# Column sums of W' moved from GpSimd to TensorE, and the output bias moved into the second lora contraction

## The chip, the core and the metric

One kernel on one core of a Trainium2 chip. The metric is the device time of one execution in microseconds, the median of several runs. The engines are TensorE (PE, with its weight loads PEld), VectorE (DVE), ScalarE (ACT), GpSimd (POOL) and SyncE (SP), which here only issues DMAs. TensorE's clock is granted at one of two levels, 1.2 and 2.4 GHz.

## What is computed

x has 64 samples of 64 channels and 1024 features, cond_128 one row per sample.

```python
h = gelu(cond @ W0 + b0); h = gelu(h @ W1 + b1)
att = softmax(h @ W2 + b2)                      # 64 x 8
agg_w = einsum('bk,koi->boi', att, weight)      # per sample 64 x 64
agg_b = att @ bias_k                            # per sample 64
c = einsum('boi,bih->boh', agg_w, x) + agg_b[:, :, None]
out = einsum('bsd,od->bso', c, W) + b
scores = c @ gate_w.T + gate_b                  # 4 ranks: 8, 16, 32, 64
sel = argmax(softmax(scores))                   # top-1, weight 1
final = c @ A[:r].T @ B[:, :r].T                # r the selected rank
y = x + out + final
```

## The kernel before

W' stands for the three weights side by side, [W.T | A.T | gate_w.T], 1024 rows and 1024 + 64 + 4 = 1092 columns, in three PSUM banks of 364 columns (`CB`). The kernel swaps the order of the two linear steps: for each of 32 tiles of 128 rows (two samples) it first computes z = x W', and then mixes the rows of z by agg_w, which is laid out as a block-diagonal 128 x 128 matrix `bd`. The bias agg_b of the mixing step then becomes, in the output, agg_b of the row times the column sums of W'.

All large contractions use fp32r operands split in a high and a low part (`xth`, `xtl`, `wh`, `wl`, `zh`, `zl`, `bd` 0 and 1): ScalarE copies the high part, VectorE subtracts it for the low part, TensorE does three passes of the four. A tile is 3 banks x 8 chunks of k x 3 passes = 72 matmuls (`main`, line 634), 9 for the mixing (`mix`, lines 653, 654, 657), 6 for lora (`lora`, lines 670 and 671) and one transpose (line 662).

The route of a tile (`route`, lines 509 to 535) adds `ubias` to the last 68 columns of the mixed z, takes the running maxima of the four scores and masks the 64 lora columns; the result in two parts, `usplit`, is transposed by TensorE, copied by ScalarE (`u_transposed`, lines 393, 394) and contracted with B in two parts (`bt_h`, `bt_l`). Of the second contraction, `ut_h1` x `bt_l`, 64 rows are lora; rows 64 to 127 of `ut_h1` are ones, and `bt_l` holds b in rows 64 (high) and 96 (low) there and zeros elsewhere. `residual` (lines 483 to 494) adds x and writes y.

GpSimd does the bias. While the chunks of W' come in it adds them up: seven additions over 128 x 1092 (line 309). The sum `wsum` is split on ScalarE (line 422) and VectorE (line 594), and six matmuls with a matrix of ones (lines 735, 736, in the second bank of tile 1) bring the column sums to all partitions; ScalarE copies them to `colsum` (line 436). Per tile GpSimd then forms `ubias` (`u_bias`, lines 322, 327) and adds the bias times 1024 columns to the x in `xin` (`x_bias`, lines 332, 337), which `residual` waits for.

Each engine has its program written out by hand, and the order is that of the text. Tile 0 is done chunk by chunk of k, as W' arrives (lines 685 to 712), with the small conditioning matmuls between (after k = 1 and after k = 4), whose results stand in banks of `p_out`. In step(0, 1), tile 1, the mixing of tile 0 stands behind k = 5, 6 and 7 of the first bank, the column sums behind k = 3 of the second, the mixing of tile 1 starts at the end of the second bank and behind k = 3 of the third, and the transpose and lora of tile 0 and the transpose of tile 1 close the third. From tile 2 on, a step has the last mixing and lora of the tile before in its first bank, and a transpose behind k = 4 of its third (9 main matmuls before the next step), for whose copies the next step waits (`s_utc`). VectorE's order ahead of the loop is: the low halves of W' (`w_lo`, line 451) with the attention softmax and its copies between, `xt_lo` of tile 1, `mixing_weights` of tile 0 (product L463, sum L466), z_lo (line 480), `bd_lo`, and lines 588 to 596. SP issues all loads of tiles 0 to 3 at once and then, in its loop, the load four tiles ahead and the store of the tile.

## Time and profile before

| | us |
|---|---|
| median of 3 runs | 508.31 |
| lowest and highest run | 507.74, 508.41 |
| the profiled execution: span from its first to its last instruction | 505.8 |
| TensorE busy | 478.2 |
| VectorE busy | 272.7 |
| GpSimd busy | 190.9 |
| ScalarE busy | 125.3 |

The times of the runs hold what lies around the span too; of the profiled execution the span is what the profile gives. In the profile, busy times add up the instructions of an engine. A matmul's row gives its pipelined duration, so that the spacing of starts tells the rate. "L634" is a line of the kernel, "<-DVE zl" in brackets who ended the idle time before an instruction. The granted clock is 1.00 at 2.4 GHz and 0.50 at 1.2 GHz.

### The profile page before, as it was taken

Reading aid. Unit: us, or ns where it says so; the run is one execution under the profiler, and the core shown is the slowest. Engines: PE = TensorE matmul, PEld = TensorE weight load, DVE = VectorE, ACT = ScalarE, POOL = GpSimd, SP = SyncE. Lnnn points to the kernel's source line nnn. Section 1 sums busy time; section 2 is a strip of 40 time slices with the busy share of each in tenths; the row PEclk is TensorE's granted clock in tenths of the full one; section 3 lists DMA queues with packets and bytes.
Section 4 is the critical chain, followed back from the end, with each engine's and each line's share of the span. In section 5 each row is a group of like instructions: output and inputs, shape, how many; then the busy total and the mean of one; then the engine's idle time right before and its main releaser. Section 6 shows DMA issues by size and latency. Waiting matters only on the chain.

```text
span 505.8 us, 8213 instructions
## 1 busy us (share of the span) xinstructions
PE 478.2 (95%) x2837; PEld 472.5 (93%) x2837; DVE 272.7 (54%) x665; ACT 125.3 (25%) x275; POOL 190.9 (38%) x149
## 2 busy tenths in 40 slices
PE   5578689999999999999999999999999999999996
PEld 4567589999999999999999999999999999999996
DVE  4999985445455544454555445445554454455523
ACT  6415112222212222222122222221222212122211
POOL 4994953333332233333322333332223333322200
PEclk9799799999999999999999999999999999999999
DMA  8940052233333223333322233333222333321002
GB/s 291 351 162 1 1 180 97 101 126 125 124 124 110 74 68 121 124 124 124 124 90 78 80 124 124 124 124 124 77 83 88 124 124 124 124 83 41 29 14 84
DMA packets 16270, 55.91 MB, mean 111 GB/s; under 512 B 2050, under 2 KB 2818, under 8 KB 16260
## 3 DMA queue, kind: packets, MB, share of 16 engines
q1 hardware_dynamic: 16116, 55.71, 31.2%
q8 instruction: 6, 0.10, 0.1%
q10 hardware_dynamic: 144, 0.07, 0.1%
q14 instruction: 4, 0.03, 0.0%
HBM read 39.00 MB, written 16.78 MB: 110 GB/s over the span
## 4 chain that ended last, share of the span: by engine, by line
PE 87%; DVE 9%; issue 1%; DMA 1%; ACT 1%; SPq 0%; POOL 0%; DVEq 0%; ACTq 0%; POOLq 0%
PE p_z L634 70%; PE p_out L653 3%; PE p_out L657 3%; PE p_out L654 3%; PE p_out L671 3%; PE p_out L670 3%; DVE wl L451 1%; DVE prod L463 1%; DVE xtl L457 1%; DMA b2r<-in_b 1%; DVE um L526 1%; PE p_out L634 1%; DVE bd L472 1%; PE p_z L662 1%; DVE xtl L558 1%
## 5 line engine op out<-in xcount | busy, mean ns | idle before, releaser
L634 PE MATMUL p_z<-wh,xth 128*128 128x364 f32 x752 | 251.5, 334 | 3.5 <-ACT wh L363 2.0
L634 PE MATMUL p_z<-wl,xth 128*128 128x364 f32 x752 | 248.0, 330 | 3.9 <-DVE wl L451 3.9
L634 PE MATMUL p_z<-wh,xtl 128*128 128x364 f32 x752 | 248.2, 330 | 0.0
L480 DVE TENSOR_TENSOR zl<-p_z,zh 128x364 fp32r<-128x364 f32 x94 | 50.4, 536 | 198.5 <-ACT zh L385 198.5
L634 PEld LDWEIGHTS p_z<-wh,xth 128*128 128x128 f32 x752 | 142.1, 189 | 5.8 <-ACT wh L363 2.2
L634 PEld LDWEIGHTS p_z<-wl,xth 128*128 128x128 f32 x752 | 141.9, 189 | 4.4 <-DVE wl L451 4.4
L634 PEld LDWEIGHTS p_z<-wh,xtl 128*128 128x128 f32 x752 | 142.4, 189 | 0.0
L327 POOL TENSOR_TENSOR ubias<-wsum,gbias 128x68 f32<-128x68 f32 x32 | 10.7, 333 | 256.8 <-DVE usplit L535 256.5
L385 ACT ACTIVATE zh<-p_z 128x364 fp32r<-128x364 f32 x94 | 44.7, 475 | 188.1 <-PE p_z L634 188.0
L337 POOL TENSOR_TENSOR xin<-xin,wsum 128x1024 f32<-128x1024 f32 x32 | 77.6, 2426 | 3.7 <-POOL wsum L332 2.3
L332 POOL TENSOR_TENSOR wsum<-colsum,aggb 128x1024 f32<-128x1024 f32 x32 | 60.7, 1898 | 0.7
L457 DVE TENSOR_TENSOR xtl<-xtin,xth 128x1024 fp32r<-128x1024 f32 x31 | 41.1, 1327 | 15.3 <-ACT xth L370 15.3
L653 PE MATMUL p_out<-zh,bd 128*128 128x364 f32 x96 | 32.2, 336 | 9.5 <-DVE zl L480 7.1
L370 ACT ACTIVATE xth<-xtin 128x1024 fp32r<-128x1024 f32 x31 | 32.9, 1060 | 1.4 <-DMA xtin<-in_xt 0.7
L657 PE MATMUL p_out<-zl,bd 128*128 128x364 f32 x96 | 31.7, 331 | 0.0
L654 PE MATMUL p_out<-zh,bd 128*128 128x364 f32 x96 | 31.7, 330 | 0.0
L393 ACT ACTIVATE ut_hl<-p_z 128x128 fp32r<-128x128 f32 x32 | 8.9, 278 | 91.5 <-PE p_z L662 91.5
L671 PE MATMUL p_out<-bt_l,ut_h 128*128 128x364 f32 (+1 forms) x96 | 31.0, 323 | 0.0
L670 PE MATMUL p_out<-bt_h,ut_hl 128*128 128x364 f32 (+1 forms) x96 | 30.3, 324 | 0.0
L377 ACT ACTIVATE bd<-aggw 64x64 fp32r<-64x64 f32 x32 | 8.2, 256 | 84.9 <-DVE aggw L466 84.9
L653 PEld LDWEIGHTS p_out<-zh,bd 128*128 128x128 f32 x96 | 18.1, 189 | 10.7 <-DVE zl L480 6.2
L490 DVE TENSOR_TENSOR wraw<-p_out,xin 128x728 f32<-128x728 f32 x31 | 28.1, 905 | 0.0
(92 smaller groups left out, 373.0 us busy)
## 6 DMA issues: line engine op xcount, KB each, us to landing
xin<-in_x SPq DMA_DIRECT2D x32, 512.0 KB, 4.5
xtin<-in_xt SPq DMA_DIRECT2D x31, 512.0 KB, 5.0
out<-wraw SPq DMA_DIRECT2D x31, 512.0 KB, 3.0
wraw<-in_wag SPq DMA_DIRECT2D x8, 546.0 KB, 7.5
bt_raw<-in_bt SPq DMA_DIRECT2D x2, 256.0 KB
xtin<-in_xt SPq DMA_DIRECT2D x1, 384.0 KB, 5.3
out<-wraw SPq DMA_DIRECT2D x2, 182.0 KB, 2.2
kern<-in_kernels SPq DMA_DIRECT2D x2, 128.0 KB, 11.1
```

The lines of the kernel that those rows point to most:

```text
L332: nc.gpsimd.tensor_tensor(bias[:, 0:O], colsum[:, 0:O], aggb[:, t, :].broadcast_to([P, O]), ALU.mult).then_inc(s_bias_x, 1)
L337: nc.gpsimd.tensor_tensor(xs, xs, bias[:, 0:O], ALU.add).then_inc(s_xb, 1)
L370: nc.scalar.activation(xth[:, j % 2, :], xtin[:, j % UNROLL, :], ACT.Copy).then_inc(s_xth, 1)
L385: nc.scalar.activation(zh[:, ring(j, m), :], z_place(i, j, m), ACT.Copy).then_inc(s_zh, 1)
L457: nc.vector.tensor_tensor(xtl[:, j % 2, :], xtin[:, j % UNROLL, :], xth[:, j % 2, :].bitcast(F32), ALU.subtract).then_inc(s_xtl, 1)
L480: nc.vector.tensor_tensor(zl[:, at, :], z_place(i, j, m), zh[:, at, :].bitcast(F32), ALU.subtract).then_inc(s_zl, 1)
L634: last = nc.tensor.matmul(z_place(i, j, m), a[:, q, k * P:(k + 1) * P], w[:, k, n * CB:(n + 1) * CB], start=k == 0 and p == 0, stop=k == K ...
L653: nc.tensor.matmul(o, bd[:, q, 0, :], zh[:, at, :], start=opens, stop=False, skip_group_check=not opens)
L654: nc.tensor.matmul(o, bd[:, q, 1, :], zh[:, at, :], start=False, stop=False, skip_group_check=not opens)
L657: nc.tensor.matmul(o, bd[:, q, 0, :], zl[:, at, :], start=False, stop=True, skip_group_check=not opens).then_inc(s_mix, 1)
L670: nc.tensor.matmul(o, ut_hl[:, :], bt_h[:, cols], start=opens, stop=False, skip_group_check=True)
L671: last = nc.tensor.matmul(o, ut_h1[:, :], bt_l[:, cols], start=False, stop=True, skip_group_check=True)
```

## The change

GpSimd's additions of W', the split of their sum, the six column-sum matmuls of tile 1 and `x_bias` go. In place of them:

- In the first loop over k, TensorE multiplies a matrix of ones with `wh` and with `wl` of each chunk, in three banks each: 3 x 2 x 8 = 48 matmuls, into the three banks that the mixing of tile 0 uses later. The conditioning results move to the one bank left free, `p_out[:, 1, 2]`.
- The column sums' 68 lora and gate columns are copied to `colsum` as before; row 0 of the other 1024 is split into `cs_h` (ScalarE) and `cs_l` (VectorE) before the mixing of tile 0 may overwrite the banks (`s_cs_lo`).
- agg_b is computed a second time in transposed form (two more small matmuls), split into `aggbt_h` and `aggbt_l`, and brought by three DMAs into rows of `ut_rows`, an array that has for each tile five rows: two of ones, two of the high and one of the low part of agg_b.
- Five row DMAs bring b (high, low) and the column sums (high, low, high) into rows 64 to 68 of `bt_l`. The second lora contraction takes 69 rows instead of 128, the last five being b and agg_b times the column sums; a third ScalarE copy per tile brings the five rows from `ut_rows` to `ut_h1`.
- `residual` adds x as it was loaded. GpSimd keeps the memsets, among them a new one of 2 x 4096, and `ubias`.
- `bt_raw` and `brow` now lie over chunks 2 and 3 of `wraw`, so that SP waits for the low half of chunk 3 before it loads B and b, and with them all loads behind; the first x load has moved ahead of that wait.
- On ScalarE `bd_hi(0, 0)` and the high parts of b and B move ahead of the first z_hi; on VectorE `bd_lo(0, 0)` and `mixing_weights(0, 1)` move ahead of the first z_lo.

The diff, cut to its core; the left-out lines declare buffers and semaphores, and remove `x_bias` and the additions whole:

```diff
...
     UNROLL = 4
-    ROW_BH, ROW_BL = 64, 96
+    ROW_BH, ROW_BL, ROW_GH, ROW_GL, ROWS = 64, 65, 66, 68, 69
...
-        bt_raw = sb("bt_raw", [P, O])
-        brow = sb("brow", [P, O])
+        bt_raw = wraw[:, 2, 0:O]
+        brow = wraw[32:33, 3, 0:O]
+        b_h, b_l = cs_h[32:33, :], cs_l[32:33, :]
...
+        ps_cond = p_out[:, 1, 2, :]
+        ps_h1 = ps_cond[:, 0:NB]
...
+        ps_aggbt = p_z[0:T, 1, 0:P]
...
                 sp.dma_start(kern[h, :, :], kernels).then_inc(s_kern_in, 16)
-            sp.wait_ge(s_clear, 2)
+            sp.wait_ge(s_clear, 1)
             sp.dma_start(gbias[:, R:RE], gate_b.partition_broadcast(P)).then_inc(s_gate_in, 16)
-            for r in (ROW_BH, ROW_BL):
-                sp.dma_start(brow[r:r + 1, :], b.rearrange("(a o) -> a o", a=1)).then_inc(s_lora_in, 16)
+            sp.dma_start(xin[:, 0, :], x_t[0]).then_inc(s_x_in[0], 16)
+            sp.wait_ge(s_wl, 4)
+            sp.dma_start(brow[:, :], b.rearrange("(a o) -> a o", a=1)).then_inc(s_brow_in, 16)
...
                 sp.dma_start(bt_raw[h, :], bt).then_inc(s_lora_in, 16)
-            sp.dma_start(xin[:, 0, :], x_t[0]).then_inc(s_x_in[0], 16)
...
+            sp.wait_ge(s_aggbt, 1)
+            for r in (ROW_GH, ROW_GH + 1):
+                sp.dma_start(ut_rows[r:r + 1, :, :], aggbt_h[:, :].bitcast(F32)).then_inc(s_gate_rows, 16)
+            sp.wait_ge(s_aggbt, 2)
+            sp.dma_start(ut_rows[ROW_GL:ROW_GL + 1, :, :], aggbt_l[:, :].bitcast(F32)).then_inc(s_gate_rows, 16)
+            sp.wait_ge(s_b_hi, 1)
+            sp.dma_start(bt_l[ROW_BH:ROW_BH + 1, :].bitcast(F32), b_h.bitcast(F32)).then_inc(s_rows, 16)
+            sp.wait_ge(s_b_lo, 1)
+            sp.dma_start(bt_l[ROW_BL:ROW_BL + 1, :].bitcast(F32), b_l.bitcast(F32)).then_inc(s_rows, 16)
+            sp.wait_ge(s_cs_hi, 1)
+            for r in (ROW_GH, ROW_GL):
+                sp.dma_start(bt_l[r:r + 1, :].bitcast(F32), cs_h[0:1, :].bitcast(F32)).then_inc(s_rows, 16)
+            sp.wait_ge(s_cs_lo, 1)
+            sp.dma_start(bt_l[ROW_GH + 1:ROW_GH + 2, :].bitcast(F32), cs_l[0:1, :].bitcast(F32)).then_inc(s_rows, 16)
...
             nc.gpsimd.memset(gbias[:, :], 0.0).then_inc(s_clear, 1)
-            nc.gpsimd.memset(brow[:, :], 0.0).then_inc(s_clear, 1)
+            nc.gpsimd.memset(ones_r[:, :].bitcast(F32), 1.0).then_inc(s_clear, 1)
             nc.gpsimd.memset(bd[:, :, :, :].bitcast(F32), 0.0).then_inc(s_clear, 1)
-            nc.gpsimd.memset(ut_h1[:, :].bitcast(F32), 1.0).then_inc(s_clear, 1)
-            nc.gpsimd.memset(ones_r[:, :].bitcast(F32), 1.0).then_inc(s_clear, 1)
...
+            pool.wait_ge(s_clear, 3)
+            nc.gpsimd.memset(ut_rows[ROW_BH:ROW_GH, :, :], 1.0).then_inc(s_clear, 1)
...
             pool.wait_ge(s_aggb, 1)
-            pool.wait_ge(s_colsum, 1)
-            pool.wait_ge(s_b_lo, 1)
+            pool.wait_ge(s_clear, 4)
+            pool.wait_ge(s_cs_hi, 1)
             u_bias(0, 0)
-            u_bias(0, 1)
-            x_bias(0, 0)
-            def step(i, j):
-                x_bias(i, j)
-                if precedes(i, j):
-                    u_bias(i, j + 1)
-            run(pool, step, 2)
+            run(pool, u_bias, 1)
...
                 nc.scalar.activation(ut_hl[:, :], src, ACT.Copy)
-                nc.scalar.activation(ut_h1[0:R, :], src[0:R, :], ACT.Copy).then_inc(s_utc, 1)
+                nc.scalar.activation(ut_h1[0:R, :], src[0:R, :], ACT.Copy)
+                nc.scalar.activation(ut_h1[R:ROWS, :], ut_rows[R:ROWS, i * UNROLL + j, :], ACT.Copy).then_inc(s_utc, 1)
...
             xt_hi(0, 1)
-            act.wait_ge(s_clear, 4)
+            act.wait_ge(s_clear, 3)
+            bd_hi(0, 0)
+            act.wait_ge(s_brow_in, 16)
+            nc.scalar.activation(b_h[:, :], brow[:, :], ACT.Copy).then_inc(s_b_hi, 1)
+            act.wait_ge(s_lora_in, 16 * 2)
+            nc.scalar.activation(bt_h[:, :], bt_raw[:, :], ACT.Copy).then_inc(s_bt_hi, 1)
...
             z_hi(0, 0, 1)
-            bd_hi(0, 0)
-            act.wait_ge(s_lora_in, 16 * 4)
-            nc.scalar.activation(bt_h[:, :], bt_raw[:, :], ACT.Copy).then_inc(s_bt_hi, 1)
+            act.wait_ge(s_colsum_mm, 1)
+            nc.scalar.activation(colsum[:, :], p_out[:, 0, 2, CB - RE:CB], ACT.Copy)
+            nc.scalar.activation(cs_h[0:1, 0:2 * CB].rearrange("p (a n) -> p a n", n=CB), p_out[0:1, 0, 0:2, 0:CB], ACT.Copy)
+            nc.scalar.activation(cs_h[0:1, 2 * CB:O], p_out[0:1, 0, 2, 0:CB - RE], ACT.Copy).then_inc(s_cs_hi, 1)
             z_hi(0, 0, 2)
-            nc.scalar.activation(bt_l[R:P, :], brow[R:P, :], ACT.Copy).then_inc(s_bt_hi, 1)
-            act.wait_ge(s_wsum, KC - 1)
-            nc.scalar.activation(wsum_h[:, :], wsum[:, :], ACT.Copy).then_inc(s_wsum_hi, 1)
...
-                    act.wait_ge(s_colsum_mm, 1)
-                    nc.scalar.activation(colsum[:, :].rearrange("p (a n) -> p a n", n=CB), p_out[:, 1, :, 0:CB],
-                                         ACT.Copy).then_inc(s_colsum, 1)
...
                 if not follows(i, j, 2):
+                    act.wait_ge(s_clear, 4)
+                    act.wait_ge(s_gate_rows, 16 * 3)
...
                 dve.wait_ge(s_lora, i * UNROLL + (j + 1))
-                dve.wait_ge(s_xb, i * UNROLL + (j + 1))
+                dve.wait_ge(s_x_in[j % UNROLL], i * 16 + 16 * (j // UNROLL + 1))
...
                 dve.wait_ge(s_stored[q], 16 * (T // 2 - 1))
-                dve.wait_ge(s_xb, T)
+                dve.wait_ge(s_x_in[slot], 16 * (T // UNROLL))
...
             nc.vector.tensor_copy(aggb[:, :, 0], ps_aggb).then_inc(s_aggb, 1)
+            nc.vector.tensor_copy(aggbt_h[:, :], ps_aggbt).then_inc(s_aggbt, 1)
+            dve.wait_ge(s_aggbt, 1)
+            nc.vector.tensor_tensor(aggbt_l[:, :], ps_aggbt, aggbt_h[:, :].bitcast(F32), ALU.subtract).then_inc(s_aggbt, 1)
...
             mixing_weights(0, 0)
-            z_lo(0, 0, 0)
-            z_lo(0, 0, 1)
-            bd_lo(0, 0)
+            dve.wait_ge(s_b_hi, 1)
+            nc.vector.tensor_tensor(b_l[:, :], brow[:, :], b_h[:, :].bitcast(F32), ALU.subtract).then_inc(s_b_lo, 1)
...
                                     ALU.subtract).then_inc(s_bt_lo, 1)
+            bd_lo(0, 0)
+            mixing_weights(0, 1)
+            z_lo(0, 0, 0)
+            z_lo(0, 0, 1)
+            dve.wait_ge(s_cs_hi, 1)
+            nc.vector.tensor_tensor(cs_l[0:1, 0:2 * CB].rearrange("p (a n) -> p a n", n=CB), p_out[0:1, 0, 0:2, 0:CB],
+                                    cs_h[0:1, 0:2 * CB].bitcast(F32).rearrange("p (a n) -> p a n", n=CB), ALU.subtract)
+            nc.vector.tensor_tensor(cs_l[0:1, 2 * CB:O], p_out[0:1, 0, 2, 0:CB - RE], cs_h[0:1, 2 * CB:O].bitcast(F32),
+                                    ALU.subtract).then_inc(s_cs_lo, 1)
             z_lo(0, 0, 2)
-            mixing_weights(0, 1)
-            dve.wait_ge(s_wsum_hi, 1)
-            nc.vector.tensor_tensor(wsum_l[:, :], wsum[:, :], wsum_h[:, :].bitcast(F32),
-                                    ALU.subtract).then_inc(s_wsum_lo, 1)
...
                     nc.tensor.matmul(o, ut_hl[:, :], bt_h[:, cols], start=opens, stop=False, skip_group_check=True)
-                    last = nc.tensor.matmul(o, ut_h1[:, :], bt_l[:, cols], start=False, stop=True,
+                    last = nc.tensor.matmul(o, ut_h1[0:ROWS, :], bt_l[0:ROWS, cols], start=False, stop=True,
...
+            def column_sums(k, w):
+                for n in range(BANKS):
+                    last = nc.tensor.matmul(p_out[:, 0, n, 0:CB], ones_r[:, :], w[:, k, n * CB:(n + 1) * CB],
+                                            start=k == 0 and w is wh, stop=k == KC - 1 and w is wl)
+                return last
+            pe.wait_ge(s_clear, 2)
...
                     main(0, 0, m, k, (0, 1))
+                column_sums(k, wh)
...
                     main(0, 0, m, k, (2,))
+                sums = column_sums(k, wl)
...
                     for d in range(2):
-                        last = nc.tensor.matmul(ps_aggb[d * C:(d + 1) * C, :], bk[:, :], attt[:, d, :],
+                        nc.tensor.matmul(ps_aggb[d * C:(d + 1) * C, :], bk[:, :], attt[:, d, :], start=True, stop=True)
+                    for d in range(2):
+                        last = nc.tensor.matmul(ps_aggbt[:, d * C:(d + 1) * C], attt[:, d, :], bk[:, :],
...
                     last.then_inc(s_cond_mm, 1)
+            sums.then_inc(s_colsum_mm, 1)
...
             pe.wait_ge(s_aggb, 1)
+            pe.wait_ge(s_aggbt, 2)
...
                         main(i, j, m, k)
+                        if first and m == 0 and k == KC - BANKS:
+                            pe.wait_ge(s_cs_lo, 1)
...
                             mix(0, 0, k - (KC - BANKS))
-                        if first and m == 1 and k == 3:
-                            pe.wait_ge(s_clear, 5)
-                            pe.wait_ge(s_wsum_lo, 1)
-                            for n in range(BANKS):
-                                cols = slice(n * CB, (n + 1) * CB)
-                                o = p_out[:, 1, n, 0:CB]
-                                nc.tensor.matmul(o, ones_r[:, :], wsum_h[:, cols], start=True, stop=False)
-                                last = nc.tensor.matmul(o, ones_r[:, :], wsum_l[:, cols], start=False, stop=True)
-                            last.then_inc(s_colsum_mm, 1)
...
                         if first and m == 1 and k == 7:
-                            pe.wait_ge(s_colsum, 1)
...
                             pe.wait_ge(s_bt_lo, 1)
-                            pe.wait_ge(s_b_lo, 1)
+                            pe.wait_ge(s_rows, 16 * 5)
...
```

## Rows read from the trace of the kernel before

**Rows 1.** The page, part 1: busy us (share), instructions

```profile
PE 478.2 (95%) x2837; PEld 472.5 (93%) x2837; DVE 272.7 (54%) x665; ACT 125.3 (25%) x275; POOL 190.9 (38%) x149
```

**Rows 2.** Waits of TensorE, 0 to 75 us: total, times, longest

```profile
PE p_out L653 <- DVE zl L480: 7.1, 3, 5.2
PE p_z L634 <- DVE wl L451: 3.9, 1, 3.9
```

**Rows 3.** Windows: stretch, us, busy (xcount) of PE, PEld, DVE, ACT, POOL; PEclk, DMA, GB/s

```profile
7.60:12.60 5.00, 4.96 (x15) 4.32 (x15) 4.90 (x6) 4.77 (x7) 3.36 (x2) 1.00 1.02 410
...
54.00:60.80 6.80, 5.24 (x18) 5.16 (x19) 6.60 (x14) 0.43 (x2) 6.39 (x6) 0.51 0.00 1
...
75.00:134.00 59.00, 59.00 (x359) 58.89 (x358) 29.35 (x81) 13.72 (x32) 20.90 (x18) 1.00 0.33 114
```

**Rows 4.** Timeline of TensorE: start us, duration, line, tiles, count, idle before

```profile
26.00 0.65 PE L709 MATMUL p_out<-attd,ones 64*64 64x256 f32 x4
...
30.80 0.50 PE L634 MATMUL p_out<-wl,xth 128*128 128x364 f32 x2
...
38.42 0.41 PE L653 MATMUL p_out<-zh,bd 128*128 128x364 f32 x1 [2.42 <-DVE bd L472]
...
44.59 0.41 PE L735 MATMUL p_out<-wsum_h,ones_r 128*128 128x364 f32 x1 [1.46 <-DVE wsum_l L594]
...
55.56 0.67 PE L653 MATMUL p_out<-zh,bd 128*128 128x364 f32 x1 [5.24 <-DVE zl L480]
...
61.92 0.43 PE L634 MATMUL p_z<-wh,xth 128*128 128x364 f32 x1
...
71.71 0.43 PE L653 MATMUL p_out<-zh,bd 128*128 128x364 f32 x1 [1.52 <-DVE zl L480]
...
77.29 0.27 PE L662 MATMUL p_z<-ident,usplit 128*128 128x128 f32 x1
...
91.81 0.27 PE L662 MATMUL p_z<-ident,usplit 128*128 128x128 f32 x1
```

**Rows 5.** Timelines of VectorE, last row GpSimd, 0 to 80 us

```profile
8.04 1.28 DVE L451 TENSOR_TENSOR wl<-wraw,wh 128x1092 fp32r<-128x1092 f32 x1
...
12.92 3.57 DVE L451 TENSOR_TENSOR wl<-wraw,wh 128x1092 fp32r<-128x1092 f32 x1
...
32.58 3.02 DVE L463 TENSOR_TENSOR prod<-kern,attp 128x512 f32<-128x512 f32 x1
...
40.22 0.68 DVE L463 TENSOR_TENSOR prod<-kern,attp 128x512 f32<-128x512 f32 x1
...
48.63 1.93 DVE L526 SCALAR_TENSOR_TENSOR um<-u,pmax 128x8 f32<-128x8 f32 x1
...
54.98 0.52 DVE L480 TENSOR_TENSOR zl<-p_z,zh 128x364 fp32r<-128x364 f32 x1
...
73.17 0.23 DVE L514 TENSOR_TENSOR u<-p_out,ubias 128x68 f32<-128x68 f32 x1
...
75.00 0.54 DVE L480 TENSOR_TENSOR zl<-p_z,zh 128x364 fp32r<-128x364 f32 x1 [0.16 <-ACT zh L385]
...
12.32 25.64 POOL L309 TENSOR_TENSOR wsum<-wsum,wraw 128x1092 f32<-128x1092 f32 x6
```

**Rows 6.** Timeline of ScalarE

```profile
17.14 1.11 ACT L363 ACTIVATE wh<-wraw 128x1092 fp32r<-128x1092 f32 x1 [0.24 <-DMA wraw<-in_wag]
...
77.85 0.26 ACT L394 ACTIVATE ut_h<-p_z 64x128 fp32r<-64x128 f32 x1
```

**Rows 7.** Groups by line and form: count, busy us, mean ns, idle before

```profile
L490 DVE TENSOR_TENSOR wraw<-p_out,xin 128x728 f32<-128x728 f32 x31 | 28.1, 905 | 0.0
...
L327 POOL TENSOR_TENSOR ubias<-wsum,gbias 128x68 f32<-128x68 f32 x32 | 10.7, 333 | 256.8 <-DVE usplit L535 256.5
...
L418 ACT ACTIVATE bt_h<-bt_raw 128x1024 fp32r<-128x1024 f32 x1 | 1.1, 1057 | 0.0
```

**Rows 8.** DMA issues: count, KB, median us to landing

```profile
gbias<-in_gate_b SPq DMA_DIRECT2D x1, 2.0 KB, 10.8
```

60 lines of the change are left out of this document (21 added, 39 removed).

## The prediction

> **What bounds the kernel now.** I read the page first: TensorE is busy 478.2 of 505.8 us, everything else half of that or less [rows 1]. So time can come only from TensorE's own work, from its clock, or from the few stretches in which it stands still. The waits of TensorE tell where those are: all of them lie before 75 us, after that none is listed, and the longest end in VectorE's hands: 7.1 us for zl, 3.9 for wl [rows 2], and in the timeline 2.42 for bd before 38.42 and 1.46 for wsum_l before 44.59 [rows 4]. From 75 us on the loop is pure TensorE: the stretch 75 to 134 is busy 59.00 of 59.00 us, and the transposes of two consecutive tiles start at 77.29 and 91.81, 14.52 us apart, for 87 matmuls and one transpose, which is 0.166 us per 364-column matmul [rows 3, 4]. Nothing that the change does to GpSimd in that loop is worth anything by itself; only the first 72 us can give.
>
> **The clock.** In the windows the stretch 7.6 to 12.6 holds 15 matmuls in 4.96 us, over 0.30 each, which is the 1.2 GHz level, although the granted clock says 1.00 there; the record seems to begin without a first entry, so I go by spacing in that stretch. After the stall of 5.24 us that ends at 55.56 the clock is 0.51 over 54.0 to 60.8, the 1.2 GHz level, and the stretch from 75 on has 1.00 [rows 3, 4]. Work that resumed at 55.56 thus ran slow for 5.3 us. The idle of 2.4 us before 38.42 cost no clock: the matmul behind it took 0.41, the one behind 55.56 took 0.67 [rows 4]. For the changed kernel, which keeps TensorE busy from 7.6 on, I estimate the rise at 7.6 + 5.3, that is 13.0.
>
> **Why VectorE is late.** The split of one chunk of W' took 1.28 us at 8.04, before GpSimd's sums had begun, and 3.57 at 12.92, while GpSimd's additions ran, six of them in 25.64 us from 12.32 on. The product of kern and attp took 3.02 at 32.58 and 0.68 at 40.22, when they had ended; one masking instruction of 8 columns took 1.93 at 48.63 beside the bias products of GpSimd [rows 5]. I read this as the two engines holding each other up, and cost VectorE in the changed kernel at its undisturbed durations.
>
> **The change, part by part.**
> First loop over k. Added: two times three column-sum matmuls for each of 8 chunks, 48 in all, so 120 instead of 72. Removed: the 3.9 us wait for wl [rows 2] and a shorter one for att. From 7.6 to 13.0 at 0.30 each some 17.5 matmuls are done; the other 102.5 at 0.166 take 17.0 us; the small conditioning matmuls in the loop take 1.2 in all (the last four instructions 0.65 [rows 4]; I add 0.55 for the rest and the two new ones, by size). The loop ends at 31.2, against 31.3 before (0.50 from 30.80) [rows 4]. W' is no limit: ScalarE split the last chunk at 17.14, for 1.11 us [rows 6]. So 48 matmuls are hidden by time that was lost before, in stalls and at half clock. Without that cover they cost 8.0 us at full clock and 14.5 at half.
>
> From the loop to the first mixing matmul. Before, it starts at 38.42 [rows 4]. In the changed kernel it waits for cs_lo, because the sums stand in the banks that it overwrites. VectorE's chain sets this. The conditioning matmuls end 75 matmuls into the loop: 13.0 + 57.5 x 0.166 + 1.2 = 23.8. Then on VectorE: the copies and the split of the transposed bias 0.9, w_lo(7) 1.2, xt_lo 1.2, product and sum 1.4: 28.5. ScalarE's two bd halves 0.5 and the b row 1.06 (1024 columns, taken as independent of the partitions): 30.1 [rows 7]. VectorE again: b_l 1.2, bt_l 1.2, bd 0.45, weights of tile 1 1.4, two z_lo at 0.45 pitch 0.9, cs_l 0.9 for 728 columns and 0.4 for 296: 36.6 (the product 0.68, z_lo 0.52, a chunk of 1092 columns 1.28 and so 1024 in 1.2, 728 columns out of PSUM 0.905) [rows 5, 7]. TensorE is ready at 31.2 + 18 x 0.166 = 34.2 and stands 2.4 us, as long as the wait for bd before, which cost no clock. The mixing starts at 36.7: **1.7 us** gained. ScalarE's cs_h rows (0.8 + 0.4, after two z_hi) are done by 33.3 and hide beside VectorE.
> The one price no row shows is GpSimd beside VectorE in that chain: its first ubias pair, two instructions of about 0.33 us [rows 7], falls at 33.3, beside the weights of tile 1. In the row at 32.58 such a product lost 2.3 us to GpSimd instructions of 4.3 us each [rows 5]; a pair of 0.33 can hold it up for 0.6 at most, and not at all if it comes behind the product. I take 0 and keep 0.6 as the other end. The Trainium skill, "SBUF — State Buffer", section "Who interferes with whom", holds that a VectorE instruction with two SBUF inputs and a GpSimd instruction that reads SBUF exclude each other for the whole instruction, so that the later one blocks; by that the gain would be 1.1 us instead of 1.7 here. The same section would leave z_lo, with one input in PSUM, undisturbed, and the trace agrees: 0.52 at 54.98, between slowed neighbours [rows 5].
>
> From the first mixing matmul to the end of tile 1 (61.92 before, so 23.5 us [rows 4]). The work left there is 69 matmuls at 0.166 (11.5), one lora contraction 0.95, two transposes 0.2: 12.7. What goes: the stall at 44.59 of 1.5 us and the six column-sum matmuls 1.0; the stall of 5.2 us at 55.56; the half clock behind it, about 2.7 us. The 5.2 us stall was the route of tile 0, whose masking ran on VectorE at 48.63 and ahead of the z_lo that started at 54.98; undisturbed a route takes 1.7 us (from 73.17 to the z_lo at 75.00, less its 0.16 of idle) [rows 5]. By my walk z_lo(0, 1, 1) ends at about 45 where TensorE asks for it at 45.4: just in time, which is the tightest point of the forecast. ScalarE's third copy for the transposed u adds 0.2 to 0.3: the wait before tile 2 becomes 0.4. Sum 13.1 instead of 23.5: **10.4 us** gained, tile 1 ends at 49.8.
> From there to the mixing of tile 2 at 71.71 (9.8 us before [rows 4]): 39 matmuls and a lora contraction, 7.4. The waits of 0.3 and 1.5 for zl go with GpSimd's x_bias. **2.4 us**.
>
> The loop. The third ScalarE copy is 5 x 128. Nearest row: 64 x 128, 0.26 us [rows 6]. The transpose starts at 77.29 and its two copies end at 78.11 [rows 4, 6]; nine matmuls stand between the transpose and the wait, so the next weight load is due at about 78.7. So 0.6 us of slack cover 0.26, for all 30 tiles; if the copy took 1.06 like the 1024-column one, 0.46 x 30 = 14 us would be lost. I take 0. The contraction over 69 rows instead of 128 streams the same columns and loads the same 128 weight columns; no row has 69. The nearest, four instructions over 64 rows with 256 columns in 0.65 us, leave 0.05 each over their columns [rows 4]. I take 0; the upper end is rival 4, a gain is excluded by the unchanged columns. The residual waits for x, which landed tiles earlier: 0.
> Queues. SP now stands until wl(3), about 14.9, with b, bt and five loads for tiles 1 to 3 behind it; before, it went on at once. W' is still arriving until 17, so this delays them by a few microseconds; bt is asked for at 30, the tile 2 load at about 37. After that SP waits in turn for aggbt, b and the sums, with eight row DMAs; queued behind them are only the load for tile 4 and the first store, due at about 50. The last row is issued at 37.3 and asked for at 47. gbias, as small, took 10.8 us to land behind a full queue [rows 8]; here the queue is empty. Cost 0; at worst 1.1 us.
> New memset on GpSimd: the row of ones (2 x 4096) takes a few us of an idle engine and is asked for at 46: 0.
>
> **Sum.** 1.7 + 10.4 + 2.4 = 14.5 us. Span 505.8 - 14.5 = 491.3. The span is 2.5 us below the median of the runs, 508.31; what lies outside it stays, so 508.31 - 14.5 = **493.8 us**.
>
> **The rivals.**
> (1) A part of the stalls stays (15%). Speaks for it: z_lo(0, 1, 1) and cs_lo come on single long chains, and every 0.1 us of VectorE counts. If 3 us remain without loss of clock the time is 496.8; if the idle again costs the clock (2.7 us more), 499.5.
> (2) The clock stays at half through the first loop (5%). The loop then ends at 7.6 + 120 x 0.30 + 1.2 = 45, the mixing starts at 48, 11.5 us later than forecast: 505.3. Against it: the rise 5.3 us after 55.56 [rows 3, 4].
> (3) The change doesn't bring VectorE back (3%): its long instructions have another cause than GpSimd. Then the stall of 5.2 us stays and 48 matmuls come on top: + 8.0, less some 2.3 of the wl stall that they fill, less 2.5 of the old sums and their wait, + 3.2: 511.5, slower. Against it: the pairs at 8.04 and 12.92, 32.58 and 40.22 [rows 5].
> (4) Slower: the 69-row contraction breaks the hiding of weight loads (3%). Place: the 96 matmuls of the second lora contraction. It decides against the change from 14.5 / 96 = 0.15 us each. A weight load takes about as long as a matmul's 0.166; with one exposed before and one behind each, 96 x 0.33 = 32 us and the time 526, with one, 510. Against it: the 0.05 us over 64 rows above.
> (5) A row DMA lands late (6%): 493.8 + 1.1 = 494.9.
> The forecast as it stands has 68%.
>
> **How the numbers follow.** The range from 491.3 (the 2.4 us wait for cs_lo gone) to 499.5 (rival 1 with its clock) takes in the forecast, rivals 1 and 5, the 0.6 us of the shared port and the 0.45 us for every us that the clock rises later. About 2 in 10 are left outside. A measurement of this kernel can tell 0.2%, 1.0 us. Faster 0.93 (the forecast and rivals 1, 2 and 5, less 0.01), the same 0.01 (rival 2 or 4 coming out between), slower 0.06 (rivals 3 and 4).
>
> **What would show it.** Right: no PE wait on wl in the first loop; matmul spacing there 0.30, then 0.166 from about 13; loop end near 31; one wait of 2 to 3 us before the first mixing matmul, put down to cs_l; no wait over 0.5 us for zl after it; granted clock 1.00 from 13 on; VectorE's split of a W' chunk at 1.28 throughout; the transposes 14.52 apart in the loop. Wrong: a loop period over 14.6 (ScalarE's copy or the 69 rows), a first mixing matmul after 38, or a second stretch at half clock.

## The result, and the profile after

| | before | after |
|---|---|---|
| median (runs), us | 508.36 (4) | 492.98 (4) |
| lowest and highest | 507.74, 508.81 | 492.56, 494.87 |
| span of the profiled execution | 505.8 | 490.4 (its own time 492.56) |

The ratio is 0.9705 (95% interval 0.9687 to 0.9723): 15.4 us less. Forecast were 493.8, and 491.3 to 499.5.

Part 1 of the page after, and two groups of its part 5, which answer to [rows 1] and to the second lora contraction:

```profile
PE 477.5 (97%) x2883; PEld 473.8 (97%) x2883; DVE 248.2 (51%) x669; ACT 133.7 (27%) x308; POOL 25.8 (5%) x76
...
L665 PE MATMUL p_out<-bt_l,ut_h 69*128 69x364 f32 (+1 forms) x96 | 30.6, 319 | 0.0
...
L664 PE MATMUL p_out<-bt_h,ut_hl 128*128 128x364 f32 (+1 forms) x96 | 29.9, 320 | 0.0
```

GpSimd went from 190.9 us busy to 25.8. TensorE has more matmuls than before and is busy no longer: up to the transpose of tile 2 it was busy 53.8 us for 267 instructions before, at a mean granted clock of 0.91, and 54.2 us for 313 after, at 1.00. The loop behind it became 1.15 us shorter, as shown below. 69 rows take what 128 rows take (319 and 320 ns).

The waits of TensorE after, for [rows 2] (total, times, longest):

```profile
PE p_out L671 <- DMA cw<-in_layer: 2.9, 1, 2.9
PE p_z L628 <- ACT wh L350: 2.6, 1, 2.6
PE p_out L647 <- DVE cs_l L587: 2.2, 1, 2.2
...
PE p_z L628 <- ACT ut_h L382: 0.3, 1, 0.3
```

The 7.1 us for zl and the 3.9 for wl are gone. What comes before the first matmul of the loop is no news; behind it the wait for `cs_l` is the only large one, and the largest of the rest is 0.3. TensorE's timeline after, the marks that answer to [rows 4]; the start of the loop over k stands first:

```profile
8.20 0.64 PE L628 MATMUL p_z<-wh,xth 128*128 128x364 f32 x1 [2.56 <-ACT wh L350]
...
9.85 0.51 PE L628 MATMUL p_out<-wh,xtl 128*128 128x364 f32 x1
...
11.06 0.48 PE L628 MATMUL p_z<-wl,xth 128*128 128x364 f32 x1
11.37 0.51 PE L628 MATMUL p_out<-wl,xth 128*128 128x364 f32 x2
11.71 0.66 PE L682 MATMUL p_out<-wl,ones_r 128*128 128x364 f32 x3
12.21 0.32 PE L628 MATMUL p_z<-wh,xth 128*128 128x364 f32 x1
...
31.38 0.33 PE L628 MATMUL p_z<-wh,xth 128*128 128x364 f32 x1
...
36.73 0.43 PE L647 MATMUL p_out<-zh,bd 128*128 128x364 f32 x1 [2.21 <-DVE cs_l L587]
...
50.24 0.43 PE L628 MATMUL p_z<-wh,xth 128*128 128x364 f32 x1 [0.34 <-ACT ut_h L382]
...
57.71 0.33 PE L647 MATMUL p_out<-zh,bd 128*128 128x364 f32 x1
...
63.19 0.27 PE L656 MATMUL p_z<-ident,usplit 128*128 128x128 f32 x1
...
483.12 0.27 PE L656 MATMUL p_z<-ident,usplit 128*128 128x128 f32 x1
```

Up to 11.37 the matmuls start 0.30 to 0.31 us apart. The two from 11.37 on take 0.17 each until the next start, the three from 11.71 on (12.21 - 11.71) / 3 = 0.167, so from 11.37 on they run at full clock: the clock rose 3.2 us after the loop began. Against before, the mark of the first mixing is earlier by 38.42 - 36.73 = 1.7, the start of tile 2 by 61.92 - 50.24 = 11.7, its mixing by 71.71 - 57.71 = 14.0, its transpose by 77.29 - 63.19 = 14.1. The last transpose of the run stood here before:

```profile
498.37 0.27 PE L662 MATMUL p_z<-ident,usplit 128*128 128x128 f32 x1
```

It is earlier by 15.25. So 1.15 us more came in 29 tiles of the steady loop: one tile took (498.37 - 77.29) / 29 = 14.520 before and (483.12 - 63.19) / 29 = 14.480 after. The last 0.15 lie in the end.

VectorE's timeline after, up to the first mixing, for [rows 5], and under it GpSimd's:

```profile
4.92 1.24 DVE L530 CAST xth<-xtin 128x256 fp32r<-128x256 f32 x1 [3.95 <-DMA xtin<-in_xt]
...
11.17 1.29 DVE L439 TENSOR_TENSOR wl<-wraw,wh 128x1092 fp32r<-128x1092 f32 x1
...
30.32 1.22 DVE L576 TENSOR_TENSOR cs_l<-wraw,cs_h 1x1024 fp32r<-1x1024 f32 x1 [1.73 <-ACT cs_h L403]
31.57 1.22 DVE L578 TENSOR_TENSOR bt_l<-wraw,bt_h 64x1024 fp32r<-64x1024 f32 x1
...
33.19 0.69 DVE L451 TENSOR_TENSOR prod<-kern,attp 128x512 f32<-128x512 f32 x1
...
35.41 0.89 DVE L585 TENSOR_TENSOR cs_l<-p_out,cs_h 1x728 fp32r<-1x728 f32 x1
36.23 0.44 DVE L587 TENSOR_TENSOR cs_l<-p_out,cs_h 1x296 fp32r<-1x296 f32 x1
```

```profile
2.50 3.50 POOL L321 MEMSET ut_rows<- 2x4096 f32 x1
33.31 0.73 POOL L328 TENSOR_TENSOR bias<-colsum,aggb 128x68 f32<-128x68 f32 x1 [27.31 <-ACT cs_h L411]
...
34.63 0.30 POOL L328 TENSOR_TENSOR bias<-colsum,aggb 128x68 f32<-128x68 f32 x1 [0.18 <-POOL ubias L333]
```

Splits of W' take 1.3 and products 0.7. The low halves of b and B stand ahead of the two that write the sums' low half (L585, L587), for which TensorE waits. The first cast took 1.24 (0.29 before), while the new memset ran on GpSimd.

### The profile page after: what moved, and what is told of

Same layout as the page of the kernel before. It is cut to its first block, busy times and chain, and to the rows that moved or that the text cites. A ratio compares the mean times of both kernels' runs of the same rounds, so it can differ in the third digit from the quotient of the medians.

```text
span 490.4 us, 8228 instructions
## 1 busy us (share of the span) xinstructions
PE 477.5 (97%) x2883; PEld 473.8 (97%) x2883; DVE 248.2 (51%) x669; ACT 133.7 (27%) x308; POOL 25.8 (5%) x76
## 4 chain that ended last, share of the span: by engine, by line
PE 95%; DVE 2%; DMA 1%; ACT 1%; issue 0%; SPq 0%; DVEq 0%; ACTq 0%
PE p_z L628 76%; PE p_out L647 3%; PE p_out L651 3%; PE p_out L648 3%; PE p_out L664 3%; PE p_out L665 3%; PE p_out L628 1%; PE p_out L682 1%; DMA wraw<-in_wag 1%; PE p_z L656 1%; DVE aggw L454 0%; DVE prod L451 0%; DVE wl L439 0%; DVE bt_l L578 0%; DVE cs_l L576 0%; DVE xtl L445 0%
## 5 line engine op out<-in xcount | busy, mean ns | idle before, releaser
L445 DVE TENSOR_TENSOR xtl<-xtin,xth 128x1024 fp32r<-128x1024 f32 x31 | 38.0, 1225 | 15.9 <-ACT xth L357 15.9
L333 POOL TENSOR_TENSOR ubias<-bias,gbias 128x68 f32<-128x68 f32 x32 | 10.6, 331 | 392.7 <-DVE usplit L523 392.5
L665 PE MATMUL p_out<-bt_l,ut_h 69*128 69x364 f32 (+1 forms) x96 | 30.6, 319 | 0.0
L454 DVE TENSOR_REDUCE aggw<-prod 128x64 f32<-128x512 f32 x32 | 22.0, 686 | 1.1
L451 DVE TENSOR_TENSOR prod<-kern,attp 128x512 f32<-128x512 f32 x32 | 21.9, 685 | 0.0
```

Source lines behind the costliest of these rows:

```text
L445: nc.vector.tensor_tensor(xtl[:, j % 2, :], xtin[:, j % UNROLL, :], xth[:, j % 2, :].bitcast(F32), ALU.subtract).then_inc(s_xtl, 1)
L454: nc.vector.reduce_sum(aggw[:, :], prod[:, :, :], AX_X).then_inc(s_aggw, 1)
L665: last = nc.tensor.matmul(o, ut_h1[0:ROWS, :], bt_l[0:ROWS, cols], start=False, stop=True, skip_group_check=True)
```

## The experiments

Ratios are against the kernel before, timed on the same chip as the experiment. "After" is the changed kernel. Theory M: VectorE is held up by GpSimd's instructions, and its delay is what TensorE waited for.

**1. Additions back.** Seven additions of W' on GpSimd, over 64 partitions and into an unused part of an array, in the kernel after.

```diff
+            for k in range(1, KC):
+                pool.wait_ge(s_wh, k + 1)
...
+                nc.gpsimd.tensor_tensor(spare[:, :], left, wh[0:C, k, :].bitcast(F32), ALU.add).then_inc(s_spare, 1)
```

> The changed kernel with seven additions over 1092 columns put back on GpSimd, beside the first loop, over wh (64 partitions, same length per partition), result unused. Theory (GpSimd and VectorE hold each other up): VectorE's split of a W' chunk goes from 1.28 us to 2 to 3.6 in places, the product for tile 0 to about 3, the wait before the first mixing matmul grows from 2.2 us by 3 to 6, the time from 493 to 496 to 500 us. Rival (VectorE's long instructions before had another cause, such as the loads still landing): VectorE's durations stay, the time stays within 0.5 us of 493.

Measured: 502.66, ratio 0.9891 (0.9870 to 0.9912). That is slower than the 496 to 500 expected. Nothing of what TensorE needs was touched, and 9.7 of the 15.4 us are gone. VectorE's timeline of this kernel, then TensorE's:

```profile
11.42 3.65 DVE L450 TENSOR_TENSOR wl<-wraw,wh 128x1092 fp32r<-128x1092 f32 x1
...
15.17 2.30 DVE L563 TENSOR_SCALAR att<-expo,sm 64x8 f32<-64x8 f32 x1
...
30.40 3.56 DVE L456 TENSOR_TENSOR xtl<-xtin,xth 128x1024 fp32r<-128x1024 f32 x1
33.88 3.04 DVE L462 TENSOR_TENSOR prod<-kern,attp 128x512 f32<-128x512 f32 x1
```

```profile
45.78 0.67 PE L658 MATMUL p_out<-zh,bd 128*128 128x364 f32 x1 [6.91 <-DVE cs_l L598]
```

The split is back at 3.65 and the product at 3.04, against 3.57 and 3.02 in [rows 5]. The first mixing is 9.05 us later than after and runs at half clock (0.67). Of the 9.05 us, 4.7 are a longer wait for `cs_l`, which stands at the end of a chain of VectorE instructions: `xtl` and `prod` alone lost 4.7 us, one behind the other. The other 4.35 had been lost before, in the first loop, where TensorE waited 1.2 us for `att` and 1.1 for wl and the granted clock was 0.87 from 13 to 20 us and 0.93 from 20 to 31. This part the expectation had not counted.

**2. Bias products back.** Per tile one multiplication and one addition over 1024 columns, on 64 partitions and into an unused part of an array.

```diff
+                nc.gpsimd.tensor_tensor(spare[:, 0:O], wh[0:C, 0, 0:O].bitcast(F32), aggb[0:C, 0, :].broadcast_to([C, O]),
+                                        ALU.mult).then_inc(s_spare, 1)
+                pool.wait_ge(s_spare, t + 1)
+                nc.gpsimd.tensor_tensor(spare[:, 0:O], spare[:, 0:O], wh[0:C, 1, 0:O].bitcast(F32),
+                                        ALU.add).then_inc(s_spare_b, 1)
```

> The changed kernel with a product and a sum over 1024 columns per tile put back on GpSimd (64 partitions, result unused, nobody waits for them). Theory: the two routes in tile 1 stretch from 1.6 us to 3 to 7, a wait for zl before the mixing of tile 1's second bank comes back with 2 to 5 us, perhaps with a stretch at half clock behind it, and the time is 496 to 502 us; the loop's period doesn't change, 14.48 us, since VectorE has slack there. Rival (the route was slow for another reason): no wait for zl over 0.5 us, 493 us.

Measured: 497.74, ratio 0.9787 (0.9766 to 0.9809), 4.8 us more than after. The timelines of TensorE and VectorE:

```profile
49.88 0.43 PE L669 MATMUL p_out<-zh,bd 128*128 128x364 f32 x1 [2.60 <-DVE zl L490]
```

```profile
40.75 2.15 DVE L482 TENSOR_TENSOR bd<-aggw,bd 64x64 fp32r<-64x64 f32 x2 [0.82 <-ACT bd L387]
...
43.39 2.98 DVE L467 TENSOR_TENSOR xtl<-xtin,xth 128x1024 fp32r<-128x1024 f32 x1
```

The wait for zl is back, within the range expected but not by the way expected: the route of tile 0 ran undisturbed here, between two GpSimd instructions; the pair `bd` (2.15 instead of 0.45) and `xtl` (2.98 instead of 1.22) ahead of it were late. From the first mixing to the transpose of tile 2 this profile takes 69.65 - 38.03 = 31.6 us, after 63.19 - 36.73 = 26.5. The difference, 5.2, is more than the waits, since the granted clock is 0.67 from 50 to 54 us. The loop behind keeps its length, (489.52 - 69.65) / 29 = 14.478 a tile, with the products in it. Each of the two kinds of GpSimd work costs time by itself, through VectorE.

**3. A nearly silent GpSimd in the kernel before.** One memset in place of the additions; the residual adds x as it was loaded. The column sums are thus those of ones, and the bias is left out of the 1024 output columns.

```diff
-            for k in range(1, KC):
...
-                nc.gpsimd.tensor_tensor(wsum[:, :], before, wraw[:, k, :], ALU.add).then_inc(s_wsum, 1)
+            nc.gpsimd.memset(wsum[:, :], 1.0).then_inc(s_wsum, 1)
...
-                x_bias(i, j)
```

> The kernel before with GpSimd's seven additions replaced by one memset and x_bias left out, so the column sums are those of ones and the output lacks the bias over its 1024 columns; the six column-sum matmuls stay where they were. Theory (the gain is VectorE's freedom from GpSimd, and the column sums on TensorE cost time): faster than the changed kernel, 486 to 489 us, VectorE's split at 1.28, no wait for zl over 0.5 us, no second stretch at half clock. Rival (the gain comes from the new place of the column sums and the new order): 500 us or more.

Measured: 486.42, ratio 0.9568 (0.9548 to 0.9587): 22 us less than before. The group of its eight splits of W', and the timeline at the one wait of TensorE that is left behind the first loop:

```profile
L427 DVE TENSOR_TENSOR wl<-wraw,wh 128x1092 fp32r<-128x1092 f32 x8 | 10.0, 1281 | 0.0
```

```profile
33.18 0.41 PE L711 MATMUL p_out<-wsum_h,ones_r 128*128 128x364 f32 x1 [1.44 <-DVE wsum_l L570]
```

GpSimd is not wholly silent: its subtraction for the low half of b ran from 29.48 for 2.40 us, and beside it `wsum_l` took 2.46, where the splits of W' of the same size take 1.28. So this last wait too has GpSimd behind it. The transposes of tile 2 and of the last tile:

```profile
55.83 0.27 PE L638 MATMUL p_z<-ident,usplit 128*128 128x128 f32 x1
...
476.93 0.27 PE L638 MATMUL p_z<-ident,usplit 128*128 128x128 f32 x1
```

All of the gain is in GpSimd's silence, and nothing of it in the new way of summing: that way costs. After is 6.6 us slower than this kernel by the medians: 7.4 at the transpose of tile 2 (63.19 against 55.83), of which the shorter loop gives 1.2 back. After has 42 more column-sum matmuls (48 for 6), 42 x 0.166 = 7.0 us; that they account for most of the 7.4 is a sum, and experiment 4 shows that leaving them out doesn't return it. A tile of the loop takes (476.93 - 55.83) / 29 = 14.521 here, as in the kernel before, so it is not GpSimd's silence that shortened the loop.

**4. Most column sums left out of the kernel after.** 6 of 48 remain, those of the last chunk, so the output has wrong column sums.

```diff
-                column_sums(k, wh)
+                if k == KC - 1:
+                    column_sums(k, wh)
```

> The changed kernel with the column sums of chunk 7 alone: 42 of the 48 matmuls of the first loop are left out, so the column sums are those of one chunk. Theory (TensorE is the bound of the changed first loop, so its added matmuls are on the path and were only paid for by the stalls that went): the conditioning matmuls end 5 us earlier and the whole of VectorE's chain with them; the first mixing matmul comes at about 30 instead of 36.7 and the time is 486 to 488. Rival (the sums ride free on waits for W'): loop end and time change by less than 1 us.

Measured: 489.87, ratio 0.9646 (0.9622 to 0.9670). 3.1 us less than after, where the matmuls left out are 7.0, and short of the 486 to 488 expected. TensorE's timeline and the windows of the 6 us behind (busy and count of PE, PEld, DVE, ACT, POOL; PEclk, DMA, GB/s):

```profile
32.44 0.43 PE L647 MATMUL p_out<-zh,bd 128*128 128x364 f32 x1 [4.19 <-DVE cs_l L587]
```

```profile
32.00:38.00 6.00, 5.56 (x24) 5.57 (x25) 3.04 (x8) 2.29 (x5) 0.00 (x0) 0.72 0.29 89
```

The first mixing is 4.3 us earlier, not 6.7 as expected: TensorE is at the barrier 6.3 us sooner (32.44 - 4.19 = 28.25, after 34.52), and VectorE isn't. The wait grew from 2.21 to 4.19, and behind it the granted clock is 0.72, which takes another part of the 4.3 back. In the kernel after, the sums are thus in part cheap because VectorE's chain is the longer one. This chain, not TensorE, sets the first mixing.

**5. 128 rows.** The rows from 64 on of both operands of the second lora contraction are zeroed beforehand; the contraction runs over all 128.

```diff
+    FULL = P
...
-                    last = nc.tensor.matmul(o, ut_h1[0:ROWS, :], bt_l[0:ROWS, cols], start=False, stop=True,
+                    last = nc.tensor.matmul(o, ut_h1[0:FULL, :], bt_l[0:FULL, cols], start=False, stop=True,
```

> The changed kernel with the second lora contraction over 128 rows again, rows 69 to 127 zero on both sides. The changed kernel's loop had a period of 14.48 us against 14.52 before, 1.2 us over 30 tiles, which the prediction had at 0. Theory: the period has nothing to do with the 69 rows; it stays at 14.48 or is 14.52 by chance, time within 0.5 us of 493. Rival: 69 rows are quicker; period 14.52, the time 494.2.

Measured: 493.09, ratio 0.9714 (0.9695 to 0.9733), one tile in 14.480. Its group:

```profile
L672 PE MATMUL p_out<-bt_l,ut_h 128*128 128x364 f32 (+1 forms) x96 | 30.5, 318 | 0.0
```

318 ns against 319: the rows cost and give nothing. Rival 4 is out, and so are the 69 rows as the cause of the shorter loop.

**6. The sums' low half first** (`e4_sums_first`). On VectorE the low halves of b and B go behind `cs_l`, on ScalarE the high half of B behind `cs_h`. VectorE's part:

```diff
             mixing_weights(0, 0)
-            dve.wait_ge(s_b_hi, 1)
-            nc.vector.tensor_tensor(b_l[:, :], brow[:, :], b_h[:, :].bitcast(F32), ALU.subtract).then_inc(s_b_lo, 1)
-            dve.wait_ge(s_bt_hi, 1)
-            nc.vector.tensor_tensor(bt_l[0:R, :], bt_raw[0:R, :], bt_h[0:R, :].bitcast(F32),
-                                    ALU.subtract).then_inc(s_bt_lo, 1)
             bd_lo(0, 0)
...
                                     ALU.subtract).then_inc(s_cs_lo, 1)
+            dve.wait_ge(s_b_hi, 1)
+            nc.vector.tensor_tensor(b_l[:, :], brow[:, :], b_h[:, :].bitcast(F32), ALU.subtract).then_inc(s_b_lo, 1)
             z_lo(0, 0, 2)
+            dve.wait_ge(s_bt_hi, 1)
+            nc.vector.tensor_tensor(bt_l[0:R, :], bt_raw[0:R, :], bt_h[0:R, :].bitcast(F32),
+                                    ALU.subtract).then_inc(s_bt_lo, 1)
```

> The changed kernel with VectorE's and ScalarE's splits of b and B moved behind the split of the column sums. Theory (VectorE's chain sets the first mixing matmul): cs_lo is ready at about 34.2, the wait of 2.2 us before the first mixing matmul goes to under 0.3, nothing later fills it, 490.8 to 491.3 us. Rival (the loop behind is where the time is made good): the wait comes back as one for zl or bd in tile 1, 493.

Measured: 490.09, ratio 0.9650 (0.9635 to 0.9664). It is faster than both kernels. TensorE's timeline, VectorE's under it:

```profile
34.42 0.33 PE L647 MATMUL p_out<-zh,bd 128*128 128x364 f32 x1
```

```profile
33.68 0.44 DVE L582 TENSOR_TENSOR cs_l<-p_out,cs_h 1x296 fp32r<-1x296 f32 x1
```

`cs_l` ends at 34.1, the wait is gone, and the mixing starts 2.3 us sooner. The last transpose stands at 480.80 instead of 483.12, also 2.3 sooner. The gain of the medians is 2.9; the 0.6 more is within the intervals and has no cause shown. The median of after doesn't hold the loss of clock that follows, but one of its runs does: three lie at 492.6 to 493.1 with a clock of 0.999 to 1.000, and one at 494.87 with 0.995. The spans of the 5 runs each of experiments 5, 9 and 10, which have the same wait, split likewise (clock 0.999 or 1.000, or 0.995 to 0.996 and about 2 us more); those of this kernel, without the wait, lie at 0.998 and 0.999 all five. Timeline and windows of experiment 9, whose profile is one of those at 0.995, at the same place:

```profile
37.35 0.67 PE L648 MATMUL p_out<-zh,bd 128*128 128x364 f32 x1 [2.24 <-DVE cs_l L588]
```

```profile
37.40:41.00 3.60, 3.60 (x13) 3.60 (x14) 0.94 (x3) 1.81 (x4) 0.00 (x0) 0.55 0.47 147
```

Against 24 matmuls in the same stretch after, at a clock of 1.00:

```profile
37.40:41.00 3.60, 3.60 (x24) 3.58 (x23) 2.03 (x5) 2.29 (x5) 0.00 (x0) 1.00 0.47 147
```

So the same wait, 2.21 or 2.24 us, in some executions costs the clock and in others doesn't.

**7. The bias rows copied before the wait for the transpose** (`e9_rows_first`), on top of experiment 6: ScalarE's third copy moves off the route.

```diff
+                nc.scalar.activation(ut_h1[R:ROWS, :], ut_rows[R:ROWS, i * UNROLL + j, :], ACT.Copy)
                 act.wait_ge(s_ut, i * UNROLL + (j + 1))
```

> As e4_sums_first, and ScalarE copies the five rows from ut_rows before it waits for the transpose, not after its two copies. Theory: the wait before tile 2 shrinks from 0.34 to under 0.1 us, nothing changes in the loop, where the slack covers the copy; 0.3 us less than e4_sums_first. Rival (the third copy costs in the loop too): more than 1 us less than e4_sums_first.

Measured: 490.38, ratio 0.9642 (0.9626 to 0.9659): not to be told from experiment 6. The wait before tile 2 fell from 0.34 in the kernel after to 0.23, not to under 0.1 as expected. It was the only wait of TensorE that named the third copy.

**8. Spare matmuls before the loop**, on top of 7: TensorE works before W' has landed, so that the clock may be up when the loop begins. First 33 of 128 columns (`e10_warm`), then 9 of 512. Both expectations count half clock up to 12.2 us, for 1.8 us; in the profile of the kernel after 10 matmuls ran slow, up to 11.4, which cost 10 x (0.305 - 0.166) = 1.4 us.

```diff
+                nc.tensor.matmul(p_out[:, 0, 0, 0:P], ones_r[:, :], ones_r[:, :], start=True, stop=True)
```

> As e9_rows_first, with 33 unused 128-column matmuls of ones by ones on TensorE between 2 and 8 us, around the first conditioning matmuls. Theory (the 13 matmuls from 8.2 to 12.2 at half clock cost 1.8 us of the path): the first loop starts at full clock, spacing 0.166 from its start, ends about 1.8 us earlier, and the time is 1.5 to 1.8 us less than e9_rows_first. Rival: W' comes in too slowly for a faster start, gain under 0.5 us, or the spare matmuls delay the conditioning: slower.

Measured: 491.93, ratio 0.9681 (0.9668 to 0.9695), 1.5 us slower than without. TensorE's timeline:

```profile
6.26 4.53 PE L672 MATMUL p_out<-ones_r 128*128 128x128 f32 x20
10.59 0.61 PE L628 MATMUL p_z<-wh,xth 128*128 128x364 f32 x1
...
15.24 0.45 PE L628 MATMUL p_z<-wh,xth 128*128 128x364 f32 x1
```

A spare matmul took 0.23 (4.53 / 20), so the loop began 2.4 us later than after's, and the clock still rose only at about 15.3, 4.7 us behind its start. Then with 512 columns, nine in all:

```diff
+                nc.tensor.matmul(p_out[:, 0, 0, :], ones_r[:, :], bd[...], start=True, stop=True)
```

> As e9_rows_first, with nine unused matmuls of 512 columns (ones by the zeroed bd) on TensorE between 2.5 and 8 us, in place of e10_warm's 33 of 128 columns, which ran 0.22 us each until 10.6 and left the clock low until 15. Theory (the half clock from 8.2 to 12.2 costs 1.8 us, and long matmuls can raise it earlier): spacing of 0.166 from 9 us or sooner, 1.2 to 1.8 us less than e9_rows_first, 489 us. Rival (the clock rises some 4 us after dense work of the real loop begins, whatever went before): no gain, or slower by what the spare matmuls delay the start.

Measured: 489.09, ratio 0.9627 (0.9614 to 0.9640), the best of all kernels that compute the whole:

```profile
5.57 2.93 PE L672 MATMUL p_out<-bd,ones_r 128*128 128x512 f32 x6
8.30 0.50 PE L628 MATMUL p_z<-wh,xth 128*128 128x364 f32 x1
...
10.94 0.33 PE L628 MATMUL p_z<-wl,xth 128*128 128x364 f32 x1
```

The loop began on time and was at full clock from 10.9, 2.6 us behind its start, and not from 9 as expected. This one profile doesn't show that the spare matmuls brought that. The delay differs by itself: without any spare matmul it was 3.2 in the profile of after, 4.7 in that of experiment 7, and between 2.9 (experiment 1, loop from 8.45) and 6.1 (experiment 10, loop from 8.58) in those of the other variants of after. The first rows at full clock of these two:

```profile
11.32 0.33 PE L639 MATMUL p_z<-wl,xth 128*128 128x364 f32 x1
```

```profile
14.69 0.33 PE L629 MATMUL p_out<-wh,xtl 128*128 128x364 f32 x1
```

The times speak for a gain: 1.3 us by the median against experiment 7, by intervals that overlap a little, and the slowest of the five runs, 489.43, lies below nine of the ten of experiments 6 and 7. Its cause is argued, not shown.

**9. A pad ahead of `kern`**, to ask whether the place of the arrays in SBUF sets the length of a tile.

```diff
+        pad = sb("pad", [P, 8])
         kern = sb("kern", [P, C, K])
```

> The changed kernel with 32 bytes per partition of unused SBUF declared ahead of kern, so that bd, usplit, ut_hl and ut_h1 begin 32 bytes further on, at the offsets modulo 64 that they have before. Theory (the loop's period of 14.48 instead of 14.52 comes from where these buffers begin): 14.52, the time 1.2 us more, 494.2. Rival (it comes from something else): 14.48 and 493.0.

Measured: 494.88, ratio 0.9730 (0.9710 to 0.9750); two of five runs were at 493.1 and 493.2. One tile took 14.487. What was expected rested on a wrong premise: the arrays stand 7744 bytes from their old places, which is 121 x 64, so by that measure they already stood at them, and the pad moved them off. The effect was 0.007 a tile, and it settled nothing. The longer median is the lost clock of experiment 6, in three of five runs, and no sign of a longer loop.

**10. No third copy from tile 2 on** (`e13_no_third_copy`). The bias rows of tile 1 then serve all later tiles. In the first two tiles the third copy stands ahead of the second.

```diff
+                if not follows(i, j, 2):
                     nc.scalar.activation(ut_h1[R:ROWS, :], ...)
```

> The changed kernel without the third ScalarE copy from tile 2 on, so that every tile keeps the bias rows of the first. Theory (the third copy costs nothing and gives nothing): period 14.48, 493.0. Rival (the later release of the next step by that copy is what shortens the period): 14.52, 494.2.

Measured: 493.12, ratio 0.9714 (0.9694 to 0.9733), one tile in 14.478. The copy costs nothing in the loop, and is not what shortened it.

**11. The arrays at the addresses of before.** `kern`, `bd`, `usplit`, `ut_hl` and `ut_h1` are brought to them by a pad and a shorter `ut_rows`, which holds the rows of one tile only; on top of experiment 10.

```diff
+        pad = sb("pad", [P, 1936])
...
-        ut_rows = sb("ut_rows", [P, T, P])
+        ut_rows = sb("ut_rows", [P, 1, P])
```

> As e13_no_third_copy, with ut_rows cut to the rows of one tile (all tiles keep the bias rows of the first) and 7744 unused bytes per partition declared ahead of kern, so that kern, bd, usplit, ut_hl and ut_h1 begin where they do in the kernel before. Theory (where these buffers lie sets the loop's period): 14.52 us per tile, the time 494.2. Rival (not their place): 14.48 us, 493.0; the cause of the 0.04 us stays open.

Measured: 495.79, ratio 0.9751 (0.9734 to 0.9769). Its transposes of tile 2 and of the last tile:

```profile
65.48 0.27 PE L658 MATMUL p_z<-ident,usplit 128*128 128x128 f32 x1
...
486.64 0.27 PE L658 MATMUL p_z<-ident,usplit 128*128 128x128 f32 x1
```

(486.64 - 65.48) / 29 = 14.523: the length of the kernel before, with the instructions of experiment 10. In 30 tiles that is 1.3 us. The other differences that could lengthen a tile are excluded: GpSimd's silence by experiments 2 and 3, which ran on one chip and show 14.478 and 14.521, and with them the chip. The pad moves every array from `kern` to `ut_h1` together, so the cause is the place of one or some of them; which one is open. The other part of its distance to after lies ahead of tile 2: its profile has the wait for `cs_l` of 2.19 with a mixing matmul of 0.67 behind it, the lost clock of experiment 6.

## Why the prediction was right

- **Start of the loop, 7.6, and rise of the clock, 13.0.** It started at 8.20: it waited for the first chunk of W', whose copy on ScalarE began when it had landed, at 6.99 instead of 6.47. That differs by itself (6.48 in experiment 9). The first cast took 1.24 beside the memset, which I had costed at 0, but it and the split behind it had ended at 6.6 and cost nothing. The clock rose at 11.4, after 3.2 us instead of 5.3, so 10 matmuls ran slow and not 17.5, 1.0 us less; the small conditioning matmuls took 1.7 instead of 1.2. That the loop ended at 31.38, forecast 31.2, is luck in part: three errors cancel. The delay of 5.3 was taken from one other place in the trace, and behind the start of this loop the profiles have 2.9 to 6.1 without spare matmuls.
- **"VectorE at its undisturbed durations".** Right: 1.29 at 11.17, 1.22 at 30.32 and 31.57, 0.69 at 33.19. Experiments 1 and 2 bring the long ones back with GpSimd's work alone, experiment 3 takes them from the kernel before. Rival 3 is out.
- **First mixing at 36.7 after 2.4 for `cs_l`.** 36.73 after 2.21. The path was right; that the start agrees to 0.03 rests on the luck of the first point. Experiment 6 shows that the order on VectorE made this wait: b and B had no reader yet.
- **GpSimd beside VectorE in that chain, 0 with 0.6 as the other end.** 0 was right. The product started first, at 33.19, and took its 0.69; GpSimd's bias product, from 33.31, took 0.73 instead of 0.30. It ended 0.16 us after the product. The Trainium skill, "SBUF — State Buffer", section "Who interferes with whom", says that whoever issues first gets the shared ports for the whole instruction; the trace agrees as to which of the two was held up, and it was GpSimd that came second, by 0.12 us. Whether it stood still for the whole product isn't clear from these rows: it ended 0.16 us behind it, and alone it takes 0.30. The forecast of 1.1 by that rule had assumed the other order.
- **Tile 1 ends at 49.8, 10.4 us.** 50.24, and 11.7 - 1.7 = 10.0. The tightest point held: no wait for zl is left. The 0.4 for the wait before tile 2 was 0.34; the third copy itself took 0.31, for 0.2 to 0.3.
- **Mixing of tile 2, 2.4.** 14.0 - 11.7 = 2.3.
- **"Loop period unchanged."** The one term that failed. 0 was forecast and 1.15 us came, plus 0.15 in the end. The prediction had looked only for what could lengthen a tile. Experiments 5 and 10 exclude the two changes that it named, experiments 2 and 3 GpSimd's work, and experiment 11 brings 14.523 back by the places of the arrays in SBUF. It more than made up for the 0.4 by which the other three terms were too high together (14.1 at the transpose of tile 2, for 14.5).
- **"As long as the wait for bd before, which cost no clock."** Right in the profile, and not in every run. Rival 1 with its clock is this in part: the run at 494.87. It doesn't show in the median of this kernel, and costs one of four runs 1.9 us.
- **48 matmuls "hidden by time that was lost before".** The sum was right. But the stalls among the time lost before were GpSimd's doing: without its work they are gone (experiment 3), and against that kernel the changed one is 6.6 us slower. Its first loop ends 7.3 us later (31.38 against 24.11), with 48 matmuls more. Leaving out 42 of them returns 3.1 (experiment 4), another order on VectorE 2.9 (experiment 6); both together weren't tried.
- Rival 2: the rise at 11.4 excludes it. Rival 5: no wait for a row of `bt_l` is in the list of waits.
